# Gated recurrence with a routed feed-forward layer: the Bm matmuls of the addend move from slot 4 to slot 5

## The reference

```python
def step(carry, xs):
    r, state = carry
    qt, kt, vt = xs
    r = decay * r + kt * vt
    retained = (qt * r).reshape(B, D)
    inp = retained @ Wi.T + bi
    gate = sigmoid(inp @ Wg.T + bg)
    blended = gate * state + (1.0 - gate) * inp
    state = tanh(blended @ A.T + inp @ Bm.T)
    out = state @ Wo.T + bo
    return ((r, state), out)

x = x + tanh(g_xattn[0]) * recurrence(layernorm(x), ctx, ctx, ...)
x = x + tanh(g_ffn[0]) * ffn(layernorm(x), ...)
# ffn: swiglu(x @ w_shared_in) @ w_shared_out
#      + sum over 2 of 8 experts of p_e * (swiglu(x @ w1_shared) @ w2[e])
```

## Time and profile before

| | |
|---|---|
| median of 3 runs | 482.32 us (481.77 to 483.99) |
| the profiled execution's own time | 483.19 us |
| its span | 481.4 us |
| mean granted TensorE clock | 0.985 of full speed |
| TensorE busy | 431.2 us |
| VectorE busy | 367.7 us |
| ScalarE busy | 221.1 us |
| GpSimd busy | 180.4 us |

### The profile page before, as it was taken

The page is one execution under the profiler, slowest core; times in us unless marked ns, Lnnn a source line. Parts: engine busy times, 40 slices in busy tenths (PEclk is TensorE's granted clock), DMA queues, the critical chain, the costliest instruction groups (busy, mean ns, idle before and its releaser), DMA issues.

```text
span 481.4 us, 12175 instructions
## 1 busy us (share of the span) xinstructions
PE 431.2 (90%) x4344; PEld 353.6 (73%) x4344; DVE 367.7 (76%) x1318; ACT 221.1 (46%) x518; POOL 180.4 (37%) x217
## 2 busy tenths in 40 slices
PE   5987699899988989999989889998999999989881
PEld 4974588777877878988778779887777676765540
DVE  2587979898989776777879768778867758556796
ACT  3564556676745454646355446453524133322100
POOL 3011302342437521102366664412635235526720
PEclk9999889999999999999999999999999999999996
DMA  6795050514234363653341199872311067696431
GB/s 159 197 246 155 2 152 3 142 31 127 52 127 115 127 127 87 137 123 80 99 123 45 45 183 217 181 148 89 124 42 46 34 127 163 142 227 193 146 113 65
DMA packets 99531, 57.05 MB, mean 118 GB/s; under 512 B 72080, under 2 KB 90000, under 8 KB 99472
## 3 DMA queue, kind: packets, MB, share of 16 engines
q1 hardware_dynamic: 95120, 44.72, 38.7%
q0 software_dynamic: 4352, 11.54, 8.1%
HBM read 23.22 MB, written 24.51 MB: 99 GB/s over the span
## 4 chain that ended last, share of the span: by engine, by line
PE 50%; DVE 29%; issue 7%; ACT 3%; POOL 3%; DMA 2%; DVEq 0%; POOLq 0%; ACTq 0%
PE bank L583 12%; PE bank L572 11%; PE bank L630 6%; PE rec L714 5%; PE rec L597 4%; DVE u_hi L1306 4%; PE bank L858 3%; DVE u_full L1308 3%; PE rec L630 2%; DVE r L1416 2%; PE rec L602 2%; PE rec L572 2%; DVE raw_w L1324 2%; ACT state L995 2%; DVE ret L1429 1%
## 5 line engine op out<-in xcount | busy, mean ns | idle before, releaser
L995 ACT ACTIVATE state<-rec 128x64 f32<-128x64 f32 x128 | 36.6, 286 | 165.3 <-PE rec L602 165.2
L1306 DVE SCALAR_TENSOR_TENSOR u_hi<-gt,state 128x64 f16<-128x64 f32 x127 | 38.8, 305 | 66.2 <-ACT state L995 65.7
L1875 POOL DMA_INDIRECT hrows<-hid_rows,slots_i x44 | 51.2, 1163 | 79.9 <-ACT state L995 45.3
L597 PE MATMUL rec<-u_hi,a_hi 128*128 128x32 f16 x512 | 47.8, 194 | 15.8 <-DVE u_hi L1306 15.7
L1888 POOL DMA_INDIRECT yg<-yrows,slots_i x44 | 45.1, 1025 | 39.9 <-ACT state L995 29.3
L597 PEld LDWEIGHTS rec<-u_hi,a_hi 128*128 128x128 f16 x512 | 37.0, 98 | 24.6 <-DVE u_hi L1306 20.0
L597 PE MATMUL rec<-u_hi,a_lo 128*128 128x32 f16 x512 | 47.4, 193 | 0.0
L1818 POOL TENSOR_TENSOR hs_lo<-hs,hs_hi 128x512 f16<-128x512 f32 x15 | 17.3, 1154 | 57.3 <-ACT hs_hi L1196 57.3
L1308 DVE SCALAR_TENSOR_TENSOR u_full<-gt,state 128x64 f32<-128x64 f32 x127 | 37.7, 297 | 0.0
L597 PEld LDWEIGHTS rec<-u_hi,a_lo 128*128 128x128 f16 x512 | 35.1, 98 | 3.0 <-issue 0.6
L602 PE MATMUL rec<-u_lo,a_hi 128*128 128x32 f16 x512 | 36.2, 194 | 0.9
(11 more groups left out here) (299 smaller groups left out, 1418.3 us busy)
## 6 DMA issues: line engine op xcount, KB each, us to landing
x_sb<-in_x_dram SPq DMA_DIRECT2D x16, 256.0 KB, 3.2
c_sb<-in_ctx_dram SPq DMA_DIRECT2D x64, 64.0 KB, 3.0
xr_sb<-in_x_dram SPq DMA_DIRECT2D x16, 256.0 KB, 3.8
hrows<-zeros SPq DMA_DIRECT2D x4, 1024.0 KB, 6.0
yrows<-squares_w SPq DMA_DIRECT2D x16, 256.0 KB, 2.8
yrows<-squares_sh SPq DMA_DIRECT2D x15, 256.0 KB, 3.0
raw_w<-in_L_ffn_w_dram SPq DMA_DIRECT2D x8, 256.0 KB, 4.4
out_dram<-raw_w SPq DMA_DIRECT2D x8, 256.0 KB, 2.4
```

The lines of the kernel that those rows point to most:

```text
L597: pe.matmul(o[:, oc, :], w[:, kc, oc * P:(oc + 1) * P], u_hi[t % 2][:, kc, :], start=False, stop=False, skip_group_check=True)
L995: act.activation(step_of(state[i % 2], t), step_of(rec[i % 2], t), ACT.Tanh, scale=1.0 / PSCALE).then_inc(st_ready, 1)
L1306: dve.scalar_tensor_tensor(out=u_hi[p][:, :, :], in0=gate, scalar=1.0, in1=old, op0=ALU.add, op1=ALU.mult).then_inc(uh_ready, 1)
L1875: pool.indirect_dma_start(hrows[q % 2], bass.IndirectOffsetOnAxis(ap=slots_i[q][:, at:at + 1], axis=0), hid_rows[t % 6][:, s, :, :].rearra ...
```

## The change

The call of `addend_bm(a, k)` moves from behind `gate_product` in slot 4 to between step 5 and `x1_transposed` in slot 5. It is made in the 14 iterations from 1 to 14 (a = 2 to 15). The start-up, which has its own calls for tiles 0 and 1, and the other engines' programs are the same.

```diff
                 recurrence(i, 4, k)
                 gate_product(a, k)
-                addend_bm(a, k)
                 duos_at(i, 4)
                 if k.dense(d):
...
                     pair(0, d)

                 recurrence(i, 5, k)
+                addend_bm(a, k)
                 x1_transposed(c, k)
```

## The result

| | before | changed |
|---|---|---|
| median | 482.50 us (481.20 to 484.56, 8 runs) | 485.39 us (484.42 to 487.54, 8 runs) |
| ratio, 95% interval | | 1.0058 (1.0036 to 1.0081) |
| profiled execution: own time, span | 483.19, 481.4 | 487.04, 485.3 |

The changed kernel is 2.9 us slower (by the interval 1.7 to 3.9 us), against +3.1 us predicted. Its profiled execution is one of its slowest, 1.65 us above its median, so the difference of the two spans (3.9 us) has to be taken apart.

A forecast was written before the change was run, and what follows sets the result against it. TensorE was taken as the bound, by its matmuls (431.2 us busy) and its waits. Losses of 1.40 and 1.90 us less a gain of 0.2 made 3.1 us on the 482.32 us median: 485.4 us, range 482.3 to 487.2.

The forecast's parts named there:

- Light iterations: Iterations 2 to 6, 9, 10: step 5 starts 1.44 us earlier, but ScalarE's queue pins step 6; gain 0.
- Iteration 1: Before step 6, where ScalarE is not the last: a gain of 0.2 us, bounds 0 and 0.22.
- u_lo in 7 and 11: Step 5's matmuls meet a late u_lo that Bm had hidden: loss 0.51 us in 7, 0.53 in 11.
- 8 and 12: Same late u_lo, but the prefix's 0.33 us wait for hots eats part of it: loss 0.18 us each.
- The bracket: The prefix's 0.33 us idle wait for hots in 8 and 12, subtracted from the 0.51 us delay.
- hid_lo: Pair 0 waits for GpSimd's hid_lo without Bm as cover: loss 1.44 us in iteration 13, 0.46 in 14.
- No absorption: Behind steps 5 and 6: later waits all start from a delayed tanh, so none of the delay is absorbed.
- Sum: Whole kernel: 1.40 + 1.90 - 0.2 = 3.1 us slower, 0.64%.
- Absorption: Rival: waits in 7 to 12 absorbed or not arising, only the hid_lo stall remains; 1.7 us, 484.0 us; chance 0.25.
- The faster outcome: Rival: light iterations' waits before step 6 go, 7.0 us; kernel 3.7 us faster, 478.6 us; chance 0.08.
- The port collision: Iteration 7: hid_rows starts 0.04 us before u_hi, which takes 1.26 us instead of 0.26; expected to repeat.
- The clock dip: Rival: standing still 1.69 us in iteration 13 brings a half-clock dip costing 1.7 us; 487.1 us; chance 0.10.

The follow-up runs named there:

- e5: Kernel before with Bm moved only in iterations 1 to 6, 9, 10, and ScalarE's step-5 tanh ahead of xn2 and gt in 5, 6, 9, 10: 0.9930.
- e8: Kernel before with Bm moved in 1 to 13, tanh first in 5, 6, 9, 10, hid_rows later in 7, 8, 11, 12, pair 0 behind Bm in 13: 0.9894.
- e7: Changed kernel with GpSimd's hid_rows started only after u_lo of step 5 in iterations 7, 8, 11, 12: 1.0009 to the kernel before.
- e9: Kernel before with only GpSimd's hid_rows put behind u_lo of step 5 in iterations 7, 8, 11, 12, Bm still in slot 4: 0.9976.
- e4: Changed kernel with pair 0 also moved behind step 5 and Bm in iterations 13 and 14: 1.0028 to the kernel before.
- e3_dense: Kernel before with Bm moved to slot 5 only in iterations 13 and 14: 1.0041.
- e6: Kernel before with only ScalarE's tanh of step 5 ahead of xn2 and gt in iterations 5, 6, 9, 10, Bm still in slot 4: 0.9986.
- e2_full: Kernel before with Bm moved to slot 5 only in iterations 7, 8, 11, 12: 1.0008.

## Why the prediction was right, and where a size was off

- **Light iterations, 0:** right. The waits of 0.77 and 0.48 us and ScalarE's queue stand as they were; e5 shows that the queue was what held step 6 in 5, 6, 9 and 10. In iteration 3 it is not the only one: VectorE's u_hi follows its slot-4 block without idle time there (I left iterations 2 and 3 out of e5 for that and didn't try it).
- **Iteration 1, -0.2:** too small. The trace has -0.28 up to step 6, which the clock's dips there blur, and from step 6 to step 7 every profile with Bm moved in iteration 1 has 3.86 us (3.89 in e8) and every one without has 4.18: another 0.32 us that I had not looked for, since I priced only the wait in front of step 6's first matmul. 0.21 of it is u_lo of step 6: its matmuls follow the step's start by 0.44 us before (65.28 to 65.72) and by 0.23 after (65.39 to 65.62).
- **u_lo in 7 and 11, 0.51 and 0.53:** measured 0.40 and 0.58. The mechanism is shown by e7. The wait is 0.52 us in 7 and 0.53 in 11, as forecast. Not forecast were the 0.08 us of the first Bm matmul and what comes back behind the transposition: in 7 the duo follows 0.44 us after its start instead of 0.62, in 11 instead of 0.47. That makes 0.42 and 0.58. In e9 the duo of iteration 7 follows after 0.47 us with Bm in slot 4, so its extra wait came with the collision; on what operand isn't settled.
- **8 and 12, 0.18 each:** the mis-sized term; measured 0.02 and 0.01. The wait for u_lo was 0.5 us as said, and the transposition is 0.60 us late with the first Bm matmul's 0.08, but the prefix had more to give than its 0.33 us. The bracket counts idle time from the modelled end of the last matmul. Counted in starts, the prefix came 0.96 us behind the transposition and can come 0.47 behind it (e9): a wait of 0.49 us. In the changed kernel, where it comes 0.44 behind, 0.52 of the 0.60 us are taken up at this place. The prediction had itself said that only distances between starts count, and then used a bracket.
- **hid_lo, 1.44 and 0.46:** measured 1.48 and 0.49. e4 shows that it is the wait.
- **No absorption:** none is shown. From step 6 of iteration 10 to step 4 of 11, where a duo waits for its rows from DRAM, the first profile has 0.22 us less than before and the repeated one 0.33 more; e3_dense has 0.31 less although nothing moved ahead of it there. From 14 to 15 it is 0.23 less and 0.06 more, and 0.28 less in e6. I take these differences as the transfers' own scatter.
- **Sum:** 3.30 us of losses were forecast and 2.98 came; of gains 0.2 was forecast and 0.60 came. That makes 2.4 us by these distances. The medians say 2.9, and 2.4 lies within their interval. So two terms were wrong by 0.3 and 0.4 us in the same direction, and that the sum of 3.1 lies so near to the median's 2.9 is in part luck; the sign and the two large terms aren't.
- **Rivals.** Absorption was the mechanism in 8 and 12 alone. The faster outcome lacked the other half of the edit: with ScalarE's order changed too (e5) it came. The port collision repeated. The rule of the Trainium skill, "SBUF — State Buffer", section "Who interferes with whom", that the order of issue decides which of the two waits, was borne out in both orders: where hid_rows started first (by 0.04 and 0.03 us in iteration 7 of the two kernels) u_hi took 1.26 us, and where u_hi started first (by 0.02 and 0.01 us in iteration 11) it took 0.28 us and hid_rows 1.29 instead of 1.16. But what the prediction made of it, that the other order would free the stall, was wrong: in iteration 11 the stall is at u_full, the next instruction on VectorE, and u_lo is as late. So nothing hung on those 0.04 us; the stall goes only when hid_rows starts behind all of u (e7, e9). The clock dip came to the tail of one execution, and in the profile of e2_full to iteration 5; in iteration 13, where TensorE stood still for 1.53 us, the granted clock stayed full in both profiles of the changed kernel.

## What to carry to other kernels

Work moved past a step of a ring makes the next step earlier only if the next engine takes the result up at once: look at what stands in front of it in that engine's queue, and move that too (0.64 us in each of four iterations with both, next to nothing with either). And what the moved work had covered is met by whoever takes its place: list every wait of the instructions behind it, with the time its operand arrives, and price those that are late; here two of fourteen iterations made two thirds of the loss. Price a wait by distances between starts, not by its idle bracket. Compare distances between fixed instructions in two traces, not spans.

## What the runs showed of the hardware

- When u_hi (0.28 us on VectorE) starts 0.03 us behind hid_rows (1.16 us on GpSimd) it lasts 1.26 us. When it starts first it lasts 0.28 us, and the instruction behind it (u_full, 0.26 us by itself) lasts 1.25 us. Putting hid_rows behind u_lo by a semaphore costs GpSimd 0.85 us of waiting and frees 1 us on VectorE.
- The first 128x256 matmul of 32-bit operands behind the 16-bit ones of a step takes 0.20 us to the next, those after it 0.12 us.
- The length of a wait alone doesn't tell whether the clock falls after it. In e2_full's profile TensorE waited 0.97 us before the transposition of iteration 5 and 0.49 us before step 6, and then ran at a granted clock of 0.78 and 0.65 of full, where the kernel before, with 0.83 and 0.48 us of waiting, kept it full. The stretch from step 6 to step 7 took 1.7 us longer. The prediction had taken iteration 5 as evidence that such waits bring none; that was one execution. In the tail, on the other hand, the clock of the changed kernel's first profile fell after a wait of 1.98 us, and e4 kept the full clock after this one of 3.00 us:

```profile
432.70 0.28 PE L630 MATMUL rec<-w_hi,raw_w 128*128 x1 [3.00 <-issue]
```

Windows of e2_full's profile, columns as above:

```profile
151.00:154.00 3.00, 2.48 (x21) 1.97 (x21) 2.69 (x10) 2.17 (x7) 2.19 (x3) 0.78 0.74 145
154.00:157.00 3.00, 3.00 (x15) 2.27 (x14) 0.84 (x5) 0.00 (x0) 0.63 (x1) 0.65 1.09 390
```

- The time until the first recurrent step differs by 1.9 us between executions of kernels that are the same there (26.4 to 28.3 us), and half-speed stretches of TensorE's clock fall at different places in iteration 1: between 0.50 and 1.00 for the window 60 to 63 us.
